# Attention scores as two float32r parts on half the TensorE array each, in a kernel of LayerNorm, routed MLPs and attention on one core

## What is computed

```python
x = x + 0.5 * _L0_ffn_ref(_layernorm(x), ...)
x = x + _L0_attn_ref(_layernorm(x), ...)
x = x + 0.5 * _L0_ffn_ref(_layernorm(x), ...)
...
def _L0_attn_ref(x, W_down, tokeys, toqueries, tovalues, W_unify, b_unify):
    xd = (x @ W_down).reshape(b, t, h, s)               # h = 16 heads, s = 16
    keys = jnp.einsum('bthk,hik->bthi', xd, tokeys) * scale
    queries = jnp.einsum('bthk,hik->bthi', xd, toqueries) * scale
    values = jnp.einsum('bthk,hik->bthi', xd, tovalues)
    dot = jnp.einsum('bqhs,bkhs->bhqk', queries, keys)
    attn = jax.nn.softmax(dot, axis=-1)
    out = jnp.einsum('bhqk,bkhs->bqhs', attn, values).reshape(b, t, e)
    return out @ W_unify + b_unify
```

## Time and profile before

| what | value |
|---|---|
| median of 3 runs | 3164.6 us |
| the profiled execution's own time | 3149.36 us |
| its span, first to last instruction | 3147.6 us |
| TensorE busy | 2916.1 us, 93% |
| VectorE busy | 2240.3 us, 71% |
| ScalarE busy | 1850.9 us, 59% |
| GpSimd busy | 745.7 us, 24% |
| mean granted TensorE clock | 0.960 |

### The profile page before, as it was taken

One profiled execution on the slowest core, in us unless ns is written; L12 is line 12 of the kernel. 1 busy time (PEld: TensorE's weight loads), 2 busy tenths in 40 slices (PEclk: granted clock), 3 DMA queues, 4 the chain that ended last, 5 costly groups with the idle time before them and its releaser, 6 DMA issues. The chain is left out here.

```text
span 3147.6 us, 57549 instructions
## 1 busy us (share of the span) xinstructions
PE 2916.1 (93%) x17263; PEld 1661.5 (53%) x17263; DVE 2240.3 (71%) x4484; ACT 1850.9 (59%) x3505; POOL 745.7 (24%) x759
## 2 busy tenths in 40 slices
PE   5999998859999999999999999999999859999987
PEld 3899998722333333333333333333333248999987
DVE  6655457548888887878887888888888376555565
ACT  5444456514666665766765666666666654444564
POOL 3353125440200300300200201101100034531353
PEclk8999999968999999999999999999999979999988
DMA  5211124231131231222212222231311052111242
GB/s 172 61 40 54 40 73 133 82 91 37 36 81 48 61 76 30 69 67 48 75 42 49 75 49 41 75 68 27 88 35 35 14 162 61 48 45 47 80 131 70
DMA packets 185826, 206.09 MB, mean 65 GB/s; under 512 B 29496, under 2 KB 149248, under 8 KB 185600
## 3 DMA queue, kind: packets, MB, share of 16 engines
q1 hardware_dynamic: 177408, 192.74, 22.7%
q0 software_dynamic: 8192, 10.57, 1.1%
HBM read 146.79 MB, written 55.66 MB: 64 GB/s over the span
## 5 line engine op out<-in xcount | busy, mean ns | idle before, releaser
L1486 DVE TENSOR_REDUCE at_mxc<-at_pb 128x1 f32<-128x512 f32 x2048 | 1297.1, 684 | 303.4 <-PE at_pb L1322 283.5
L1466 ACT ACTIVATE at_ex<-at_pd 128x512 f32<-128x512 f32 x2048 | 1099.6, 597 | 557.5 <-PE at_pd L1331 557.1
L1322 PE MATMUL at_pb<-at_ka,at_qa 96*128 96x512 bf16 x2048 | 802.0, 392 | 40.8 <-DMA at_qa<-at_scr 18.2
L1331 PE MATMUL at_pd<-at_qa,at_ka 99*128 99x512 bf16 x2048 | 779.9, 383 | 25.0 <-DMA at_qa<-at_mparts 19.7
L768 DVE TENSOR_TENSOR f_ml_hl<-f_ml_h,f_ml_hh 128x512 fp32r<-128x512 f32 (+1 forms) x384 | 288.1, 752 | 425.6 <-ACT f_ml_hh L844 424.6
L1322 PEld LDWEIGHTS at_pb<-at_ka,at_qa 96*128 96x128 bf16 x2048 | 200.2, 98 | 695.4 <-DVE at_mxc L1486 496.0
L1340 PE MATMUL at_po<-at_ex,at_va 128*32 128x512 f32 x4096 | 553.2, 610 | 9.6 <-DVE at_os L1574 5.6
L841 ACT ACTIVATE f_ml_h<-f_ml_pL,b1T 128x512 f32<-128x512 f32 (+1 forms) x384 | 244.1, 636 | 451.9 <-PE f_ml_pL L895 448.5
L910 PE MATMUL f_ml_pA<-f_wh,f_ml_hh 128*128 128x256 f32 (+1 forms) x1408 | 409.6, 291 | 0.0
L912 PE MATMUL f_ml_pA<-f_wl,f_ml_hh 128*128 128x256 f32 (+1 forms) x1408 | 402.1, 286 | 0.0
L913 PE MATMUL f_ml_pA<-f_wh,f_ml_hl 128*128 128x256 f32 (+1 forms) x1408 | 402.0, 286 | 0.0
(11 more groups left out here) (143 smaller groups left out, 2981.2 us busy)
## 6 DMA issues: line engine op xcount, KB each, us to landing
f_wraw<-in_L_ffn_w SPq DMA_DIRECT2D x128, 256.0 KB, 2.8
at_scr<-at_parts SPq DMA_DIRECT2D x96, 256.0 KB
at_ka<-at_scr SPq DMA_DIRECT2D x64, 256.0 KB, 5.2
at_qa<-at_scr SPq DMA_DIRECT2D x64, 192.0 KB, 3.9
f_ro_xr<-in_L_attn_x SPq DMA_DIRECT2D x16, 512.0 KB, 3.9
f_ml_xr<-in_L_attn_x SPq DMA_DIRECT2D x16, 512.0 KB, 4.2
x<-f_ml_yo SPq DMA_DIRECT2D x16, 512.0 KB, 4.0
at_xr<-x SPq DMA_DIRECT2D x16, 512.0 KB, 4.7
```

What stands on the lines that cost most here:

```text
L1322: eng.matmul(pb[place(c)][:, :], qa[g][0:KROWS, qh, j, qt * P:(qt + 1) * P], ka[g][0:KROWS, j, kh * 512:(kh + 1) * 512], start=True, stop= ...
L1331: eng.matmul(pd[place(c)][:, :], ka[g][0:KROWS + MROWS, j, kt * P:(kt + 1) * P], qa[g][0:KROWS + MROWS, qh, j, :], start=True, stop=True). ...
L1466: eng.activation(ex[t % 2][:, j, :], pd[place(GH * t + j)][:, :], ACT.Exp).then_inc(s_ex.sem, 1)
L1486: eng.tensor_reduce(mxc[:, c % CH:c % CH + 1], pb[place(c)][:, :], AX.X, ALU.max).then_inc(s_mx.sem, 1)
```

## The change

Queries and keys are split into two float32r parts in place of three bfloat16 ones. A score's contraction is then over three slots of 16 rows (48; with two maximum rows 50), which fits into half of the array's 128 rows. The four heads of a group stand as two pairs: heads `e = 0` on partitions 0 to 63, heads `e = 1` on partitions 64 to 127. In the built program each score product has a tile of 64 rows x 128 columns of the array, at row 0 or at row 64; before, each had the whole array.

- A **maximum tile** is two heads: `for_max` issues two products, one in each half, into the two banks of a `pb` (two `pb` of two banks each, in place of three of one). One `tensor_reduce` (`maximum`) takes both maxima, over 2 x 512 columns. A step has 2 of them in place of 4.
- **Exponentials and side tasks share a ring** of three banks `pd` (class `Ring`); the bank `px` is gone. A product waits until the bank's occupant of three places ago is read; a side task also waits until the side task before it has been read.
- **The order of a step** is new: the side task's product stands before the third score product, `times_v` before the fourth; the VectorE part of a side task stands in the same step, behind both maxima.
- **GpSimd's part of the split is gone**: VectorE writes the second part itself (`side_out`, with `parts` and `mparts` as target). `negate` becomes a `tensor_tensor` maximum (`both_halves`), and the sign moves into the split of the maxima.
- **DMA**: the parts take 8 bytes per element in DRAM (before 6), in 4 KB rows (before 2 KB); per batch 8 stores in place of 12. A unit is loaded with 12 issues in place of 10, half a unit's maxima with 4 in place of 3.

```diff
-SLOTS = 6
-Q_PARTS = [0, 1, 2, 0, 1, 0]
-K_PARTS = [0, 0, 0, 1, 1, 2]
-KROWS = SLOTS * HS
+Q_SLOTS = [0, 0, 1]
+K_SLOTS = [0, 1, 0]
+KROWS = len(Q_SLOTS) * HS
+MROWS = 2
+HALF = P // 2
+RING = 3
...
+class Ring:
...
+    def full(self, n):
+        return n + 1 + self.per * self.i
+
+    def before(self, n):
+        return n // RING + self.per // RING * self.i
+
+    def freed(self, n):
+        return n // RING + 1 + self.per // RING * self.i
...
-            def scores_for_max(b, g, c):
-                qh, j, qt, kh = c // CH, c % CH // NT, c % NT // 2, c % 2
-                if c == 0:
+            def for_max(b, g, t, kh):
+
+                qh, p, qt = t // NT, t % NT // 4, t % 4
+                if t == 0 and kh == 0:
                     eng.wait_ge(s_ld[g].sem, s_ld[g].at(16 * ULOADS * (b + 1)))
...
+                eng.wait_ge(s_mx.sem, s_mx.at(2 * (ST * unit(b, g) + t) + kh - 1))
+                for e in range(2):
+                    rows = slice(HALF * e, HALF * e + KROWS)
+                    mm = eng.matmul(pb[kh][:, e * NQ:(e + 1) * NQ], qa[g][rows, qh, p, qt * P:(qt + 1) * P],
+                                    ka[g][rows, p, kh * NQ:(kh + 1) * NQ], start=True, stop=True)
+                mm.then_inc(s_b.sem, 1)
+
+            def for_exp(ring, b, g, t, j, n):
+
+                qh, kt, e, p = t // NT, t % NT, j % 2, j // 2
...
+                eng.wait_ge(s_free[n % RING].sem, s_free[n % RING].at(ring.before(n)))
+                rows = slice(HALF * e, HALF * e + KROWS + MROWS)
+                eng.matmul(pd[n % RING][:, :], ka[g][rows, p, kt * P:(kt + 1) * P], qa[g][rows, qh, p, :],
+                           start=True, stop=True).then_inc(s_full.sem, 1)
...
+            def side_product(ring, a):
+                bank = pd[a.n % RING]
+                eng.wait_ge(s_free[a.n % RING].sem, s_free[a.n % RING].at(ring.before(a.n)))
+                if a.after is not None:
+                    eng.wait_ge(s_free[a.after % RING].sem, s_free[a.after % RING].at(ring.freed(a.after)))
...
+                    if ahead:
+                        for_max(b1, g1, t, 0)
+                    for j in range(2 if tiles else 0):
+                        for_exp(self.ring, *coming, j, tiles[j])
+                    if ahead:
+                        for_max(b1, g1, t, 1)
+                    if a:
+                        side_product(self.ring, a)
+                    if tiles:
+                        for_exp(self.ring, *coming, 2, tiles[2])
+                    times_v(self.ring, b, par, g, t, done)
+                    if tiles:
+                        for_exp(self.ring, *coming, 3, tiles[3])
...
+            def maximum(b, g, t, kh):
+                eng.wait_ge(s_b.sem, s_b.at(2 * (ST * unit(b, g) + t) + kh + 1))
+                eng.tensor_reduce(mxc[:, t // NT, kh, t % NT::NT], pb[kh][:, :].rearrange("p (e k) -> p e k", e=2),
+                                  AX.X, ALU.max).then_inc(s_mx.sem, 1)
```

More of the change, by code:

```diff
@@ L1203, in phase, with place, exps @@
+            def place(self, task, b, par, g):
+                n = self.ring.take()
+                a = Place(task, b, par, g, n, self.ns + self.dns, self.side)
+                self.side = n
+                self.ns += splits(task)
+                return a
+            def exps(self, do, b, g, t, now_t, **k):
+                self.ready = [self.ring.take() for _ in range(GH)]
+                do.lead(b, g, self.ready)
             def phase(self, do, b, par, g, prev=True, last=False):
-                before = None
@@ L1205, in phase @@
                 for t in range(ST):
-                    task = task_at(g, t, prev, last)
-                    now, n, ns = None, self.n, self.ns
+                    done = self.ready[-1]
+                    ends = last and g == 3
+                    b1, g1 = next_unit(b, g)
+                    coming = (b, g, t + 1) if t < ST - 1 else (b1, g1, 0)
+                    tiles = None
+                    if not (ends and t == ST - 1):
+                        tiles = self.ready = [self.ring.take() for _ in range(2)]
@@ L1218, in phase @@
-                    do.step(b, par, g, t, n, ns, before, now, last)
-                    before = now
-        def place(c):
-            return 1 if c == ST * GH - 1 else c % BANKS
-        def back(c):
-            return next(d for d in range(1, ST * GH) if place((c - d) % (ST * GH)) == place(c))
-        unit = lambda b, g: 4 * b + g
-        next_unit = lambda b, g: (b, g + 1) if g < 3 else (b + 1, 0)
+                        a = self.place(task, b, par, g)
+                    if tiles:
+                        tiles += [self.ring.take() for _ in range(2)]
@@ L1231, in attention @@
+                    do.step(b, par, g, t, coming, tiles, done, a, side, not ends, last)
         block = ctx.enter_context(nc.Block())
@@ L1275, in _, with before, first, lead @@
             class Do:
-                def start(self, tasks):
+                def before(self, sides):
                     load_rows(0)
+                    qk = [a for a in sides if a.kind == "qk"]
+                    eng.wait_ge(s_row, 8)
                     for c in range(DT):
-                        store_parts(0, c, len(QK) // 2 * (c + 1))
+                        store_parts(self.ring, 0, c, qk[4 * c + 3].n)
                         load_unit(0, c)
-                    load_maxima(tasks[-1])
-                def step(self, b, par, g, t, n, ns, before, now, last):
+                def first(self, a):
+                    load_maxima(self.ring, a)
+                def lead(self, b, g, tiles):
+                    pass
+                def step(self, b, par, g, t, coming, tiles, done, a, side, ahead, last):
                     if t == 0:
@@ L1418, in _, with end @@
+                def end(self, sides):
+                    for a in sides:
+                        side_product(self.ring, a)
             Walk(eng, Do())
```

451 lines of the change are left out of this document (213 added, 238 removed).

## The result

| | before | after |
|---|---|---|
| median of 4 runs each | 3166.1 us | 3202.4 us |
| lowest and highest | 3164.4, 3168.4 us | 3185.8, 3214.4 us |
| the profiled execution's own time | 3149.36 us | 3197.88 us |

The account below looks back on a forecast made before the run. TensorE's order of products was taken to set the pace, VectorE close behind. Eight batches of 190 us (1523 in place of 1766) and -6 us gave 2900, with the median's 15 us 2915, rounded to 2920 us; own range 2840 to 3000, wider one to 3090.

Parts of the forecast that it names:

- rival A: Score products: the two array halves do not overlap; plain step 2.93 us, total time 3285 us, slower; chance 0.08.
- C: Attention loop: VectorE sets everything, 172 us a batch, total time 2775 us; chance 0.05.
- Rival B: Score products: halves overlap only in part, 0.30 us a pair; plain step 2.5 us, total time 3050 us; chance 0.17.
- The chain between them.: Attention loop, TensorE to VectorE and back through the maximum tiles: 3.1 us for a step with a side task.
- the ring's third bank leaves little slack, for which I add 3 us a batch: Attention loop: ScalarE's exponentials, 2.06 us a step, do not decide; the three-bank ring costs 3 us a batch.
- I keep the 5 us per batch; bounds 0 and 12: Once a batch, TensorE's stall behind SyncE's stores of the parts stays at 5 us.
- scaled by bytes: DMA: a batch's two halves, from first issue to the loads behind them, go from 24 to 32 us.
- Together -6 us: First stage: GpSimd's split removed and first maxima going from 38 to 36 us save 6 us.
- Rival D: TensorE's clock falls; plain step 4.0 us at 0.50; 3230 us with a quarter of steps there; chance 0.04.
- the bounds of the side step: Attention loop: a step with a side task takes 2.9 to 3.3 us, 3.1 in the forecast.
- waits of score products on freed banks larger than those on maxima (ring): Profile after the change: a sign that would show the forecast wrong, with the ring holding TensorE; no size given.

Follow-up runs that it names:

- e5: Changed kernel with all score products on the first half of the array's rows, so none can overlap: 3535.0 us, plain step 3.06 us.
- e2: Changed kernel with each maximum tile reduced over one head's 512 columns, the other head's maxima set to 0: 3135.3 us, plain step 2.61 us.
- e1: Changed kernel with exponentials over 256 of a tile's 512 columns: 3148.4 us, plain step 2.39 us.
- e3: Changed kernel with the second maximum tile of a step cut to one head, the freed bank left unused: 3146.7 us, plain step 2.61 us.
- e4: As e3, but with the freed bank as the ring's fourth: 3001.8 us, plain step 2.18 us.
- e7: Changed kernel with SyncE's store wait and next unit's load moved behind the load of the maxima: 3139.8 us, ratio to before 0.995.
- e8: Changed kernel with first-stage memsets behind the LayerNorm powers, and side tasks waiting for the task before the last where allowed: 3181.6 us, ratio to before 1.013.
- e6: Changed kernel with the side task's product moved behind the fourth score product: 3226.95 us, ratio to before 1.024.

## Why the prediction was wrong

**Right.** The halves overlap fully: groups of two 0.23 us apart make 0.115 us a product, as taken. The Trainium skill ("TensorE: Matmul & The Clock Gate", Part 3, packing small matmuls) has a speedup of 3.07 for four tiles of 32 rows, by which the sum would have risen by 143 us; two tiles of 64 rows show no such loss here. A reduction over 1024 columns comes 1.14 us after the one before (2.36 less the last one's 1.22), where 1.13 was worked out. e5 shows a plain step without the overlap (3.06 us, 2.93 in rival A), and e2 excludes C. Rival B's plain step of 2.5 us does not follow from its own pitch, which gives 8 x 0.15 + 1.09 = 2.29.

**The step that failed is "The chain between them."** It followed the maximum tiles from TensorE to VectorE and back and dismissed the ring with "the ring's third bank leaves little slack, for which I add 3 us a batch". The ring's chain is what sets a plain step, as e1, e3 and e4 show. It can be added up from the profile of the kernel before: 1.00 for the values' product, then the latency to ScalarE (0.42 in the earlier trace rows, 0.54 measured after the change), 0.60 for an exponential, and the way from the third score product to the values' product (0.31 in the earlier trace rows, 0.42 measured). The exponential stands on the page of the kernel before:

```profile
L1466 ACT ACTIVATE at_ex<-at_pd 128x512 f32<-128x512 f32 x2048 | 1099.6, 597 | 557.5 <-PE at_pd L1331 557.1
```

With the old numbers the chain is 2.33 us, above TensorE's 2.01 and VectorE's 2.26, and with the measured ones 2.61. I took busy time for ScalarE's part (2.06 us) where latency counted. For a `qk` step the same chain gives 3.35 with the old numbers (1.02 more) and measures 3.66, where 3.1 was forecast, because the change puts the side product between the freed bank and the values' product.

How far would the chain alone have carried the forecast? With the old numbers a batch is 44 x 3.35 + 20 x 2.33 + 8 = 202 us, and the forecast some 3010 us: inside the 2840 to 3090 us and still faster than before. With the measured latencies it is 44 x 3.66 + 20 x 2.61 + 8 = 221 us, a loop of 1770 us, as long as before. So the overlooked chain accounts for some 90 us of the loop's miss, and some 150 us come from latencies: from a score product that stands alone to its reader and to the values' product 0.1 us more pass than from one in the dense row of the kernel before, and none of the rows that I had taken showed that.

**What each term measured.** By medians over six batches a batch is 225 us where 190 were forecast; the same medians of the kernel before make 224. The 225 are 17 plain steps at 2.61 (forecast 2.3, so 5 us more), two more without a side product at 3.9 (one with `f`'s read, one behind the stall; 3 more), 44 with one at 3.69 on the mean (3.1, 26 more), and the stalled step of 11.0 (2.3 + 5 + 3 = 10.3, about equal). The 3.69 holds `xd` and `u` steps of 4.5, which the kernel before had too, and distances with `f`'s read of up to 4.9, where the kernel before had 3.3 to 3.9 for its `f` steps. That the mean lies so near the `qk` step's 3.66 is partly chance. Plain steps gained 0.25 us each on before; steps with a side task lost 0.09 us on the mean (3.60 before), and the stall took the rest back.

**The stall.** "I keep the 5 us per batch; bounds 0 and 12" was too low: 8.7 us over a plain step on the mean of seven, inside the bounds. The 5.0 were also too much for the kernel before, since the earlier trace rows happened to show the longest of its seven stalled steps; their mean is 3.3 us over a plain step, so the stall grew by 5.4 us a batch, 38 us in all. The 32 us "scaled by bytes" for stores and loads were 30.1 (1340.98 to 1371.07). e7 shows that the order on SyncE's queue is the cause: with the maxima first, the step is a plain one in all batches.

**The first stage.** "Together -6 us" was +23.3. The memsets that now stand ahead of the powers, and the wait of each side task on the one before it, were not counted at all, though the changed program shows both. e8 gets 20.3 of it back, and what is left is still 3 us later than before, so the gain of 6 us did not come either.

**The clock.** Rival D was given 0.04, and a part of it came true. The changed kernel has 134 us more of the loop at the lower level than before (172 against 38). A plain step takes 4.07 us there in place of 2.60, so that of each us at the lower level 0.36 are lost; the 134 us are worth some 48, an estimate. D's price was close (4.0 us for a plain step at 0.50), but not its shape. In the changed kernel each of the twelve falls within the loop comes with TensorE idle for over a microsecond: at the stall seven times, three times while VectorE reads `f` (1.2 us), and twice at `g = 0`, `t = 15` (2.3 and 2.5 us, no cause shown; the kernel before has these two as well). With no gap of that kind it fell in the last unit of e3, e6, e7 and e8, where a step has fewer products, which is nearer to what D had in mind; why it did not fall in the changed kernel's own last unit stays open.

The range missed the time (3202 against 3090), since neither a ring chain nor a late first stage was among the rivals, and the bounds of the side step (2.9 to 3.3) were drawn around one chain alone. One sign of being wrong did name it, "waits of score products on freed banks larger than those on maxima (ring)": in the changed kernel the weight loads of the score products wait 164 us for ScalarE over the loop, and those of the maximum tiles 22 us for VectorE.

## What to carry to other kernels

When buffers are turned over by three engines, add up every closed chain (start of a product, latency to its reader, the reader's time, the freed bank's next product, and all that stands behind that product in program order) and compare it with the busy times; the longest of them sets the step. Here one more bank for the last product of a step was worth more than a faster product (0.43 us a step in e4 against nothing in e3), and moving one item out of one chain needs the chains of its readers checked as well. A change that halves the work in a loop is also a change of what arrives late: count the new one-time work and look at the queue whose stores were hidden by the old pace.

## What the runs showed of the hardware

- Two float32r products on rows 0 to 63 and 64 to 127 start within 0.01 us of each other and run at 0.23 us for both; each weight load of 0.19 us is hidden (changed kernel, 1401.25 to 1401.83).
- From the start of a lone score product to the values' product on four column tiles 0.42 to 0.43 us pass, its own record being 0.50 us; where it follows others its record is 0.40 us and the distance 0.33 us (e1, 1359.01 to 1359.34).
- From the start of a lone score product to the start of ScalarE's exponential 0.54 us pass (1401.25 to 1401.79); from the end of the exponential to the next product in the bank 0.05 us.
- The granted clock fell to 0.50 while TensorE waited for DMA and stayed there for over 10 us at full activity; in e5 it stayed for up to 82 us with TensorE counted as busy. In the last unit of e7 it fell where TensorE's longest idle stretch was 0.45 us in 2.60, and stayed down for 30.7 us; plain steps went from 2.60 to 4.07 us.
